# An attention and expert block on one core: the hand-over from the last attention row to the first expert products, reordered on four engines

## What is computed

```python
# attention: 16 heads of 8 channels, causal, relative keys and values
att = einsum('bhtd,bhsd->bhts', q, k) * scale + einsum('bhtd,tsd->bhts', q, rk)
att = softmax(where(causal, att, -inf))
y = einsum('bhts,bhsd->bhtd', att, v) + einsum('bhts,tsd->bhtd', att, rv)
x = x + y @ w_proj
# experts: on the layernormed tokens xt
scores = softmax(xt @ gate_w.T)
idx = top_k(scores + gate_bias, 2)
for e in range(8):
    h = silu(xt @ w1[e].T) * (xt @ w3[e].T)
    y = y + gate_e[:, None] * (h @ w2[e].T)
z = silu(xt @ sw1.T) * (xt @ sw3.T) @ sw2.T      # two shared experts
x = x + y + z
```

## Time and profile before

| | us |
|---|---|
| median of three runs | 788.38 (786.87 to 790.86) |
| the profiled execution | 783.03 |
| its span, first to last instruction | 781.2 |
| PE busy | 699.7 (90%) |
| DVE busy | 593.5 (76%) |
| ACT busy | 517.5 (66%) |
| POOL busy | 255.9 (33%) |

### The profile page before, as it was taken

One profiled execution on the slowest core, in us unless ns is written; L12 is line 12 of the kernel. 1 busy time (PEld: TensorE's weight loads), 2 busy tenths in 40 slices (PEclk: granted clock), 3 DMA queues, 4 the chain that ended last, 5 costly groups with the idle time before them and its releaser, 6 DMA issues. The chain is left out here.

```text
span 781.2 us, 27135 instructions
## 1 busy us (share of the span) xinstructions
PE 699.7 (90%) x10368; PEld 506.4 (65%) x10368; DVE 593.5 (76%) x2036; ACT 517.5 (66%) x1032; POOL 255.9 (33%) x253
## 2 busy tenths in 40 slices
PE   4567879999888899987999988997999999999997
PEld 3345557777666677765777766776666666666665
DVE  8856668888687788877888788887467776776676
ACT  3476877788797778896888898887425334443331
POOL 9343345444346433544633445633000000000000
PEclk9897979999999999999999999999999999999999
DMA  9998998889899878678778769951000000000000
GB/s 303 294 235 293 331 286 264 274 222 286 286 262 290 274 223 261 224 237 244 228 204 268 225 201 274 280 171 49 3 22 28 28 0 28 28 15 1 13 15 14
DMA packets 116687, 140.32 MB, mean 180 GB/s; under 512 B 8848, under 2 KB 83088, under 8 KB 116368
## 3 DMA queue, kind: packets, MB, share of 16 engines
q1 hardware_dynamic: 116560, 138.59, 58.0%
HBM read 82.26 MB, written 56.30 MB: 177 GB/s over the span
## 5 line engine op out<-in xcount | busy, mean ns | idle before, releaser
L1047 DVE CUSTOM_DVE_ANT_0 ps<-ps,near 128x128 f32<-128x128 f32 (+3 forms) x512 | 245.2, 511 | 90.7 <-PE ps L818 57.7
L972 ACT ACTIVATE work<-ps,nmin 128x128 f32<-128x128 f32 (+3 forms) x512 | 249.9, 542 | 65.1 <-DVE nmin L1047 58.4
L830 PE MATMUL ps<-ident,work 128*128 128x128 f32 x1280 | 203.4, 278 | 12.0 <-issue 8.7
L830 PEld LDWEIGHTS ps<-ident,work 128*128 128x128 f32 x1280 | 157.5, 143 | 35.5 <-issue 14.4
L818 PE MATMUL ps<-kb,qb 128*128 128x128 bf16 (+3 forms) x512 | 131.6, 310 | 15.2 <-ACT work L972 11.1
L776 POOL TENSOR_SCALAR_AFFINE_SELECT work<-work 128x512 f32<-128x512 f32 x96 | 61.5, 641 | 238.8 <-ACT work L961 203.5
L1364 ACT ACTIVATE near<-ps 128x512 f32<-128x512 f32 x80 | 47.7, 596 | 134.7 <-PE ps L1329 134.6
L780 POOL TENSOR_TENSOR work<-work 128x512 f32<-128x512 f32 x96 | 124.2, 1293 | 8.0
L1032 DVE COPY work<-ps 128x512 f32<-128x512 f32 (+1 forms) x192 | 123.4, 643 | 3.1 <-PE ps L830 1.5
L1339 PEld LDWEIGHTS ps<-work,near 128*128 128x128 f32 x640 | 82.6, 191 | 34.3 <-issue 31.7
L961 ACT ACTIVATE work<-ps 128x512 f32<-128x512 f32 (+1 forms) x160 | 90.3, 564 | 13.8 <-PE ps L830 13.2
(11 more groups left out here) (110 smaller groups left out, 629.1 us busy)
## 6 DMA issues: line engine op xcount, KB each, us to landing
near<-w_slots SPq DMA_DIRECT2D x96, 512.0 KB, 5.4
w_slots<-relS SPq DMA_DIRECT2D x128, 256.0 KB, 4.7
qk_rows<-work SPq DMA_DIRECT2D x36, 256.0 KB, 5.1
near<-w_slots SPq DMA_DIRECT2D x32, 256.0 KB, 4.9
w_slots<-near SPq DMA_DIRECT2D x8, 512.0 KB, 6.1
qk_rows<-y SPq DMA_DIRECT2D x9, 256.0 KB, 3.3
qb<-qk_rows SPq DMA_DIRECT2D x24, 96.0 KB
kb<-qk_rows SPq DMA_DIRECT2D x24, 96.0 KB
```

The lines of the kernel that those rows point to most:

```text
L830: ins = nc.tensor.transpose(tp_ps[:, m % 2, n * P:(n + 1) * P], prob[:, m % PROBS, n * P:(n + 1) * P], ident[:, :])
L972: ins = nc.scalar.activation(prob[:, m % PROBS, h * wide:(h + 1) * wide], qk_ps[:, m % 3, h * wide:(h + 1) * wide], ACT.Exp, bias=nmin[:, ...
L1047: nc.vector.tensor_tensor_reduce(out=scores, in0=scores, in1=near[:, q % NEAR, a, 4 * P - wide:4 * P, r], scale=1.0, scalar=3e38, op0=ALU. ...
```

## The change

The root for the first 24 token tiles and the exchange of tables around it go from slot 352 into the last row: on ACT behind the exponential of unit 328, on DVE in slot 330. On ACT `normalise` of chunk 0 goes one slot ahead, to slot 352. On PE the wait for the readers of the three banks and the gate scores go from before the experts into the first step of `last_row`, which is behind the first hidden layer of chunk 0. `rv` of pair 15 goes from bank 7 to bank 6 and no longer waits for the reader of the scores; the second `yt`, which uses bank 7, waits for it in its place. Bank 6 is wanted by the products of the experts, so a wait for the reader of `rv` (`near_values`) is put at step 2.

```diff
@@ schedule
-    bank.update({("rv", e): highest, ("yt", e, 0): lowest, ("yt", e, 1): highest, ("yb", e): lowest, ("pj", e): highest})
-    before.update({("yt", e, 1): ("rv", e), ("yb", e): ("yt", e, 0), ("pj", e): ("yt", e, 1)})
+    bank.update({("rv", e): highest - 1, ("yt", e, 0): lowest, ("yt", e, 1): highest, ("yb", e): lowest, ("pj", e): highest})
+    before.update({("yb", e): ("yt", e, 0), ("pj", e): ("yt", e, 1)})
@@ PE
                 wait_copied(pe, NU - 1)
-                for kind, *what in LAST:
-                    pe.wait_ge(*READ[kind](*what))
-                experts["scores"](pe, 0)
 
                 def last_row(step):
 
                     e = GI - 1
                     if step < 2:
                         if step == 0:
-                            experts["wait_scores"](pe, 0)
+                            for kind, *what in LAST:
+                                pe.wait_ge(*READ[kind](*what))
+                            experts["scores"](pe, 0)
                         for c in range(RVN // 2 * step, RVN // 2 * (step + 1)):
                             rv(e, c)
                     if step in (2, 3):
                         if step == 2:
                             experts["wait_turned"](pe, 0)
+                            pe.wait_ge(rvn_done, GI)
+                        else:
+                            experts["wait_scores"](pe, 0)
                         yt(e, step - 2)
@@ ACT
                     if m < NU:
                         exp(m)
+                    if m == FIRST[NQ - QUADS] + 8:
+                        experts["roots"](act, 0)
                     if m == NU:
-                        experts["roots"](act, 0)
-                    if m == NU + 1:
                         experts["normalise"](act, 0)
@@ DVE
-                    if m == NU:
+                    if m == FIRST[NQ - QUADS] + 10:
                         experts["inverse"](dve, 0)
```

## The result

| | before | after |
|---|---|---|
| median of ten runs, us | 789.51 (786.87 to 794.83) | 785.15 (782.43 to 795.75) |
| profiled execution, us | 783.03 | 782.59 |
| its span, us | 781.2 | 780.9 |

The change makes the kernel faster: ratio 0.9921, 95% interval 0.9895 to 0.9946 (medians alone: -0.55%). The ratio leaves out one slow run of the changed kernel (795.75), the medians do not. The forecast was 784.6 us in 781.9 to 788.4, or -0.48%. Direction and range hold; the gain is larger than the one that I held likeliest.

What follows compares the result with a forecast made beforehand. PE was taken to bound the last row, with an idle, half-clock seam behind it. Seam gain 4.88 us (2.37 + 1.34 + 0.93 + 0.24) less 1.1 in the row gives 3.8: median 784.6 us from 788.38, range 781.9 to 788.4.

Steps and rivals of the forecast that it cites:

- Row: Last attention row: table exchange for the roots on ACT delays PE at `yb` 13, losing 1.1 us.
- rival (c2): Last row: each table switch takes twice its time in the experts, PE loses 4.0 us; 787.5 us, 6%.
- Rival (a): Last row: PE's 1.1 us are lost where it would have waited anyway; 783.5 us, 15%.
- Seam without the clock: Seam between last row and experts: earlier normalising 2.37, avoided wait 0.93 and shorter scores 0.24 us gained.
- the normalising: Seam, ACT: `normalise` comes right behind the copy, without load and root ahead of it, 2.37 us earlier.
- the wait: Seam, PE: expert products run instead of waiting for the copy of the value products, 0.93 us gained.
- the scores: Seam, PE: gate scores take 0.79 us behind the expert products, not 1.03, gaining 0.24.
- The clock: Seam, PE: clock stays at 1.00, so the turn and 32 value products run fast, 1.34 us gained.
- Rival (b): Seam: clock falls nonetheless after 0.98 us of idleness, 1.34 + 0.24 us not gained; 786.2 us, 17%.
- rival (c): Row and seam: clock falls twice and ACT's 2.9 us absence reaches PE; 1.3 us slower, 789.6 us, 7%.
- step 2: PE's added wait for `near_values` before the turning of y costs nothing, some 1.5 us of cover staying.
- (d): Roots come no earlier, or the gain dies in the `near_values` wait or DVE's queue; half remains, 787 us, 5%.

Runs made afterwards that it cites:

- e4: Changed kernel with the first square root replaced by a plain pass, so no exchange of tables (output not the block's); row 31.23 us, ratio to before 0.9932.
- e9: e7 with the roots behind exponential 332 instead of 328 and the inverse in slot 334; row 32.26 us, ratio to before 0.9934.
- e2: Kernel before with only the roots in the last row and the earlier normalising, PE's order and banks kept; seam 16.68 us, ratio to before 0.9954.
- e10: Kernel before, unchanged, profiled again; seam 20.21 us with 3.4 us at half clock, no ratio given.
- e5: Kernel before, unchanged, submitted as an experiment; seam 21.84 us with 6.8 us at half clock, ratio 1.0015.
- e11: Kernel before, unchanged, profiled once more; seam 21.71 us with 6.8 us at half clock, no ratio given.
- e7: Changed kernel with the wait for the last residual moved from step 6 to step 8; h03 to end 216.69 us, ratio to before 0.9914.
- e3: Changed kernel with roots, inverse and normalising put back, keeping only PE's new order and banks; seam 20.46 us, ratio to before 0.9971.

## Why the prediction was right, and where its size was off

- **Row.** 1.1 us foretold, 1.25 measured (1.22 of them at `yb` 13, with its wait for `rel` 126 in its place); e4 puts all of it on the exchange of tables, e9 moves the wait by moving the exchange. The pair of loads and the root took 2.94 us from the end of exponential 328 (515.62) to the start of 329 (2.93 foretold). The longer switch that the Trainium skill gives (ScalarE: Activation LUTs, What ACT_TABLE_LOAD costs: 2.66 us with its drain) did not show: each load took 1.28 us and its activation followed 0.01 to 0.02 us later. That is rival (c2) gone. Rival (a), the row swallows it, is gone by the row's 32.48.
- **Seam without the clock.** Foretold 4.88 - 1.34 = 3.54; measured 18.65 - 15.02 = 3.63. 2.37 were for the normalising (2.39: it starts 0.47 after the copy's start and not 2.86) and the remaining 1.24 are the order's (1.24 by e2 too; foretold 0.93 + 0.24). That these two add up is luck: the wait gave 1.16 and not 0.93, the scores nothing and not 0.24.
- **The clock.** This is the term that was mis-sized. I took 1.34 from one profile, in which the turn and the value products ran slow. It cost 1.16 us there and 1.23 in e10, and 2.7 us in e5 and e11, where it also reached the scores and the first expert products. The changed kernel idles 0.96 us and kept 1.00 through the seam in both of its profiles (and so did e2, e4 and e7 to e9): all of it is gained. Rival (b) and rival (c) fall with that. The prediction read the fall as one 3.35 us after PE had gone idle; the other profiles don't bear out such a figure (last section).
- **The sum.** Without their halts the four profiles of before have a mean seam of (19.81 + 21.36 + 19.88 + 21.38) / 4 = 20.61 us. Against 15.02, less 1.25 in the row, that is 4.3 us, -0.55%, an estimate, since four executions don't tell how often the clock is low for the longer time; the forecast of 3.8 was low by one term. The two ratios of the changed kernel, -0.79% (-1.05 to -0.54) and -0.65% (-0.94 to -0.37), both take it in. Whether anything beyond it is real stays open: no stretch shows it, and the ratios can't tell 1 us.
- **Nothing at step 2.** The added wait for `near_values` cost nothing: `yt` starts in the flow of products (562.00 in the changed kernel), and DVE's transposition ends at 560.74 there, so 1.3 us of cover are left where some 1.5 were foretold. (d) falls; half of the 3.8 would have given 786.5, not the 787 that stands there.
- **Chances.** I held a gain within 0.5% likelier (0.53) than one beyond it (0.40). It came out just beyond, because the clock's smaller size had put the likeliest case on the inner side of the edge.

The version of e7 beats both kernels: by its stretches 1.8 us less than the changed one; its ratio to before is 0.9914 (0.9881 to 0.9947). With the roots at unit 332 (e9) another 0.2 by the row, which its ratio of 0.9934 (0.9897 to 0.9970) can't show.

## What to carry to other kernels

Where one engine idles for some microseconds at a seam, price the clock as well as the wait, and from several profiles: the wait was 3.36 us each time, the time at half clock 3.4 or 6.8. Effects of a few microseconds in a span whose beginning scatters by ten are read from fixed landmarks around the change; a comparison of spans would have shown 0.3 us here. An exchange of tables in a saturated stretch can cost less than its length (1.25 and 1.03 us here, of 2.94), but look for the buffer that the stalled engine has still to release, and put a protecting wait at the step where the buffer is next written, not where its work ends.

## What was not expected of the hardware

In four profiles of the same program PE idled 3.35 to 3.37 us ahead of the turn, and each time the granted clock fell; but it fell between 0.4 us before the turn's start (e10) and 1.3 us behind it (e5, e11), which is 3.0 to 4.7 us after PE had gone idle, and it stayed at half for 3.4 us in two and 6.8 us in the other two. In e3, with the same idle time of 3.36 us, it fell 1.9 us after PE had gone idle and stayed at half for 6.8 us. In the seven profiles with 0.96 us of idleness there it did not fall. With 24 small transposes in the idle time (2.78 us of work, 0.66 us left idle) it did not fall either, in one profile. What sets the moment of the fall stays open.
